# Layer-1 pairs of GpSimd, the order of TensorE's pairs and the spread of the gathers in a recommender tower

## The reference, cut to what matters

```python
e = stack([tbl_f[ids[:, f]] for f in range(32)], axis=1)        # 1024 x 32 x 16
xk = e
for W in (W0, W1, W2):                                           # K = 64 outputs each
    xk = relu(einsum('bmd,bhd,mhk->bkd', e, xk, W)); outs.append(xk.sum(axis=2))
h = concat([*outs, dense_ctx], axis=1)
h = relu(h @ W_top1 + b_top1); h = relu(h @ W_top2 + b_top2); y = h @ W_top3
```

## Time and profile before

| | |
|---|---|
| time, median of 3 runs | 665.63 us (664.72 to 666.06) |
| the profiled execution | 662.89 us, its span 661.1 us, so 1.8 us lie around the span |
| TensorE (PE) busy | 605.5 us (92%) |
| VectorE (DVE) busy | 569.6 us (86%) |
| GpSimd (POOL) busy | 453.1 us (69%) |
| ScalarE (ACT) busy | 358.0 us (54%) |
| mean granted TensorE clock | 0.974 |
| DMA, mean over the span | 181 GB/s |

### The profile page before, as it was taken

The page is one execution under the profiler, slowest core; times in us unless marked ns, Lnnn a source line. Parts: engine busy times, 40 slices in busy tenths (PEclk is TensorE's granted clock), DMA queues, the critical chain, the costliest instruction groups (busy, mean ns, idle before and its releaser), DMA issues. The chain is left out here.

```text
span 661.1 us, 9151 instructions
## 1 busy us (share of the span) xinstructions
PE 605.5 (92%) x3172; PEld 247.5 (37%) x3172; DVE 569.6 (86%) x336; ACT 358.0 (54%) x669; POOL 453.1 (69%) x307
## 2 busy tenths in 40 slices
PE   4499849979999999989999999999999999999988
PEld 3352313224343344424343344434443443434434
DVE  5759975986989899897989899898989898999863
ACT  0184922817647392927647392928556482829251
POOL 6786887888869694888869697787877070716220
PEclk9689969989999999999999999999999999999989
DMA  6899679797695969698694969688795869492000
GB/s 186 190 240 278 150 213 214 217 216 193 146 248 142 208 199 214 193 200 237 141 255 137 213 193 211 193 198 225 180 258 131 186 217 217 155 214 41 1 0 1
DMA packets 60175, 119.82 MB, mean 181 GB/s; under 512 B 15271, under 2 KB 33734, under 8 KB 60054
## 3 DMA queue, kind: packets, MB, share of 16 engines
q1 hardware_dynamic: 41798, 111.02, 67.1%
q10 hardware_dynamic: 10768, 6.53, 3.7%
q0 software_dynamic: 7584, 1.96, 3.0%
HBM read 115.27 MB, written 5.25 MB: 182 GB/s over the span
## 5 line engine op out<-in xcount | busy, mean ns | idle before, releaser
L483 DVE TENSOR_TENSOR z_dve<-xq,x0b 128x2048 f32<-128x2048 f32 x209 | 464.5, 2283 | 68.4 <-ACT xq L637 39.2
L879 PE MATMUL acc<-z_dve,w_cin 128*64 128x512 f32 x1672 | 379.2, 597 | 11.1 <-DVE z_dve L483 10.8
L439 POOL TENSOR_TENSOR z_pool<-x0b,xs 128x2048 f32<-128x2048 f32 x47 | 213.5, 4558 | 108.2 <-ACT xs L637 107.2
L423 POOL DMA_INDIRECT emb<-in_tbl_dram,ids_all x224 | 220.0, 982 | 72.0 <-issue 70.3
L879 PEld LDWEIGHTS acc<-z_dve,w_cin 128*64 128x64 f32 x1672 | 122.4, 137 | 234.9 <-issue 186.5
L645 ACT ACTIVATE xq<-acc 32x512 f32<-32x512 f32 x256 | 144.6, 565 | 3.4
L637 ACT ACTIVATE xq<-acc 64x512 f32<-64x512 f32 x128 | 73.0, 570 | 119.8 <-DVE z_dve L483 62.8
L879 PE MATMUL acc<-z_pool,w_cin 128*64 128x512 f32 x376 | 90.6, 615 | 16.1 <-POOL z_pool L439 16.1
L637 ACT ACTIVATE xs<-acc 64x512 f32<-64x512 f32 x128 | 75.7, 591 | 1.9
L483 DVE TENSOR_TENSOR z_dve<-xq,x_rot 128x2048 f32<-128x2048 f32 x30 | 67.2, 2281 | 0.0
L879 PE MATMUL acc<-z_dve,w_sym 128*64 128x512 f32 x256 | 58.0, 593 | 0.2 <-DVE z_dve L483 0.2
(11 more groups left out here) (97 smaller groups left out, 229.2 us busy)
## 6 DMA issues: line engine op xcount, KB each, us to landing
x0b<-x0t SPq DMA_DIRECT2D x120, 512.0 KB, 14.5
x_rot<-x0t SPq DMA_DIRECT2D x60, 512.0 KB, 6.2
x_rep<-x0t SPq DMA_DIRECT2D x15, 512.0 KB
x0b<-x0t SPq DMA_DIRECT2D x16, 256.0 KB, 7.2
emb<-in_tbl_dram,ids_all POOLq DMA_INDIRECT x224
x0t<-emb_t ACTq DMA_DIRECT2D x28, 128.0 KB
w_cin<-in_L_rec_W_dram SPq DMA_DIRECT2D x16, 64.0 KB
x_lo<-x0t SPq DMA_DIRECT2D x15, 64.0 KB
```

The lines of the kernel that those rows point to most:

```text
L423: nc.gpsimd.indirect_dma_start(out=rows[:, D * f:D * f + D], out_offset=None, in_=tables[f], in_offset=bass.IndirectOffsetOnAxis(ap=ids_al ...
L439: nc.gpsimd.tensor_tensor(z_pool[:, n % ZP_SLOTS, :, :], x0b[b % 2][:, 2 * j:2 * j + 2, :], xs[l - 1][:, :].unsqueeze(1).broadcast_to([P, ...
L483: nc.vector.tensor_tensor(z_dve[:, base % Z_SLOTS, :, :], in0.unsqueeze(1).broadcast_to([P, 2, N]), in1, ALU.mult).then_inc(z_made, 1)
L879: ins = nc.tensor.matmul(acc[l][K * side:K * side + K, :], weights[c], z[:, c, NH * side:NH * side + NH], start=start and c == 0, stop=sto ...
```

## The change

GpSimd has no pair of layer 1 in block 0 and only (NAT, 0) in block 1. Its gathers are spread anew. TensorE takes the SWP pairs of layer 1 first. The waits that count `xs_x1_ready` follow from there being no such write for block 0. Two pieces of tile 1's transposing move in block 0: the second half's transposes to the third pair of layer 2, and ScalarE's `move_half(1, 1)` ahead of `set_relu(1, 0, 0)`.

```diff
     def pool_l1(b):
-        return (3,) if b == 0 else (0, 1)
+        return () if b == 0 else (0,) if b == 1 else (0, 1)
     def gathers(b):
-        return (9, 1, 12) if b == 0 else (0, 14, 8) if b == 1 else (0, 14, 2)
+        return (14, 2, 8) if b == 0 else (3, 9, 6) if b == 1 else (0, 10, 6)
     def l1_order(b):
         if b == 0:
-            return [(NAT, 0), (NAT, 1), (NAT, 2), (SWP, 0), (SWP, 1), (SWP, 2), (NAT, 3), (SWP, 3)]
-        return [(NAT, 0), (NAT, 1), (SWP, 0), (SWP, 1), (SWP, 2), (SWP, 3), (NAT, 2), (NAT, 3)]
+            return [(NAT, 0), (NAT, 1), (NAT, 2), (NAT, 3), (SWP, 0), (SWP, 1), (SWP, 2), (SWP, 3)]
+        if b == 1:
+            return [(SWP, 0), (SWP, 1), (NAT, 0), (SWP, 2), (SWP, 3), (NAT, 1), (NAT, 2), (NAT, 3)]
+        return [(SWP, 0), (SWP, 1), (NAT, 0), (SWP, 2), (NAT, 1), (SWP, 3), (NAT, 2), (NAT, 3)]
...
                 n1, n2, n3 = gathers(b)
-                pool.wait_ge(xs_x1_ready, b + 1)
+                if b > 0:
+                    pool.wait_ge(xs_x1_ready, b)
...
                     if not last:
                         x1_pool(t, k + 1)
+                    if k == 0 and first_tile:
+                        move_half(1, 1)
...
                         x1_swp(t, k + 1)
                         if k == 1:
                             set_relu(0, t, 2)
-                    if k == 0 and first_tile:
-                        move_half(1, 1)
...
             x1_nat(0, 0)
             x1_swp(0, 0)
-            x1_pool(0, 0)
             set_relu(0, 0, 0)
...
                         cin_pair(2, t, k, v, j, i)
-                        if i == 6 and k == 0 and first_tile:
+                        if i == 2 and k == 0 and first_tile:
                             pe.wait_ge(emb_copied, 1)
                             transpose_half(1, 1)
```

More of the change, by code:

```diff
@@ L500, in add_relu @@
                 if l == 0:
-                    dve.wait_ge(xs_x1_ready, 2 * t + 2)
+                    dve.wait_ge(xs_x1_ready, 2 * t + 1)
                     dve.wait_ge(x1_ready[NAT], 2 * t + 2)
@@ L663, in x1_pool @@
                 act.wait_ge(*acc_done(0, t, k))
-                if blk(t, k) > 0:
+                if blk(t, k) > 1:
                     act.wait_ge(*pool_made(1, t, k - 1))
@@ L863, in claim @@
                 if l == 0:
-                    pe.wait_ge(xs_x1_ready, 2 * t + k)
+                    if blk(t, k) > 1:
+                        pe.wait_ge(xs_x1_ready, 2 * t + k - 1)
                     pe.wait_ge(x1_ready[NAT], 2 * t + k)
```

## The result

| | before | after |
|---|---|---|
| time, median | 665.85 us (664.72 to 667.13, 4 runs) | 690.39 us (688.87 to 690.57, 4 runs) |
| span of the profiled execution | 661.1 us | 688.8 us |
| mean granted TensorE clock | 0.974 | 0.960 |

The change makes the kernel slower: the ratio is 1.0373, with a 95% interval of 1.0349 to 1.0396. That is +24.5 us in the medians and +27.7 us between the two profiled executions; the forecast was +19.4. Runs that add a line above these have them one higher.

What follows compares the result with a forecast made beforehand. TensorE, 92% busy and nearly gapless from block 3, was taken as the bound. Opening -8.8, blocks 4, 8, 10, 12 +21.6, block 6 +6.2 and block 14 +0.4 sum to +19.4 on 665.6: 685.0 us, range 671 to 691.

Steps and rivals of the forecast that it cites:

- The opening: Blocks 0 to 2: TensorE's 1.23 and 8.74 us holes go, and -8.8 us remains of all the opening.
- Rival 3: The opening gives nothing because VectorE or a late x0b holds block 1, and the waits stay: 694 us; chance 0.06.
- Place, cause and number of the waits: Even blocks, second half's transposes: the last gather starts 7.5 us later and lands late during the x0b load; 4.3 us wait.
- the sign: In the profile after: waits of 3.5 to 5 us on gathers' DMA, tiles of 77.5 to 79.5 us, half-clock stretches behind each.
- The landing: Time from a gather's start until it lands during the x0b load: 7.8 to 8.7 us, taken as 8.4.
- Rival 1: The gathers land in time, under 4.1 us, so the kernel is faster: 652 us; chance 0.12.
- The slow clock behind each wait: After each wait at the transposes TensorE's clock is lowered: 1.1 us a time, bounded by 0 and 1.7.
- Block 6: GpSimd's 8.04 us stall in block 5 recurs: two late layer-1 pairs, a 4.4 us gather wait and the clock, +6.2 us.
- What was costed at nothing: The pairs' order in layer 1 costs nothing; `move_half(1, 1)` fits in ScalarE's queue, and nothing waits for the SyncE loads it advances.

Runs made afterwards that it cites:

- the filled wait: The changed kernel with ten matmuls of 256 columns on constants ahead of each of the six waits: 678.38 us, against 689.10 for the changed kernel on that chip.
- the last spread of the gathers: The changed kernel with gathers spread (14, 3, 8), (5, 9, 7), (0, 10, 6), 64 ahead of block 2: 718.18 us on the second chip, 647.53 on the third.

## Why the prediction was right, and which term was too small

The forecast was 685.0 us, with 671 to 691 around it; 690.39 is inside, near its upper end. That it is inside is in part luck: the sum itself missed 8.3 us of the 27.7 between the profiled executions, and the forecast's base of 665.6 plus 27.7 would be 693.3, outside. The mechanism is the one that was forecast. The steps in turn:

- **The opening**: the hole of 8.74 us and the one of 1.23 go, as said. Layer 1 of block 1 ends on TensorE at 103.5 us, where 102.7 was forecast, and block 2's at 146.29, where it was 144.8. So -7.3 us remains instead of -8.8. Of the 1.5 us missing, 0.8 is block 1's later end, 0.1 the path from there to the transposes (39.0 us, forecast 38.9), and 0.6 the clock (142.50 to 146.29 is 3.79, forecast 2.14 + 1.1). Rival 3, an opening that gives nothing, is out. (Two of the forecast's sums here are 0.1 us too high: 84.75 + 15.4 + 0.6 is 100.75 and not 100.85, and 66.1 + 2.32 + 2.40 + 4.60 is 75.4. It changes nothing.)
- **Place, cause and number of the waits**: six, in blocks 2, 4, 6, 8, 10 and 12, at the second half's transposes, released by the gathers' DMA. In blocks 4, 8, 10 and 12 they are 4.44, 4.53, 4.58 and 4.43 us, against 4.3 forecast; in block 2 it is 5.06. The tiles of 79.5 to 80.0 us lie above the 77.5 to 79.5 that were named as the sign. The path from the odd block's layer 1 to these transposes was forecast as 38.9 us and took 39.2 (426.56 to 465.79). The landing was taken as 8.4 us, and is 8.8. Rival 1, gathers that land in time, falls in that row.
- **The slow clock behind each wait**: this is the term that was mis-sized. It stood with 1.1 us a time. Each of the four tiles is 6.44, 6.58, 6.70 and 6.15 us longer than before; less its wait that leaves 2.00, 2.05, 2.12 and 1.72, mean 2.0, and the filled wait gives 1.6 to 1.8 in a measurement of its own. I had allowed for a part of the low stretch to fall into the wait and taken the upper bound from a single pair (1.7). In fact next to nothing of it did: from the start of the transposes to that of the pair it is 0.62 us (before: 0.37), and the whole pair behind them ran slowly, 3.5 us to the next start in blocks 4, 8 and 10 and 3.1 in block 12 (before: 1.8). The low clock took in the start of layer 0 too, 4.64 us in block 4 and 3.92 in block 10 for 3.60, but that cost the tile almost nothing: from this row to the next layer 0 it is 36.7 us, against 36.6 before, since TensorE has a wait of 0.7 us for VectorE to give up in layer 2. The clock makes 3.5 of the 4.3 us by which these four tiles exceed the forecast's +21.6; the longer waits make the rest.
- **Block 6**: +8.5 us against the forecast's +6.2. GpSimd's 8 us stall recurred (8.25 us), at the gather that was named. GpSimd was 5.1 us late behind it, as forecast (its two layer-1 pairs start 22.1 us after the start of layer 0 in block 5, at 262.76; those of block 10 start 17.0 us after that of block 9, at 426.56). The late pairs cost less than said, 0.67 and 0.86 us and not 2.8 in all: the slack of each was larger than I took it to be. The wait for the gather is 6.46 us and not 4.4: I had taken its landing to end with the `x0b` load, but it starts at 298.31 and TensorE is released at 305.83, 7.5 us later and some 3 us after that load thins out (DMA share 0.67 in 302 to 304 and 0.18 in 304 to 306, windows of PE). The run with two gathers later supports this: there the load is issued at 285.86 instead of 282.03 and the gather starts 5.5 us later (303.83), and the release comes at 309.49, 23.6 us after the load's issue where it was 23.8. So in this block the landing went by the load and not by its own start. What takes the last 3 us isn't known.

```profile
302.00:304.00 2.00, 0.00 (x0) 0.81 0.67 126
304.00:306.00 2.00, 0.17 (x1) 0.50 0.18 34
```

- **What was costed at nothing**: TensorE's order did cost nothing (0.999 alone). `move_half(1, 1)` moved forward has no run of its own; the only loss seen there is the 0.8 us by which block 1 ends late.

Together: 1.5 us for the opening, 4.3 for the four tiles and 2.3 for block 6 are missing in the forecast. They account for 8.1 us of the 8.3 between +19.4 and the +27.7 of the profiled executions; the medians lie 3.2 us closer together than these two. The term that was too small is thus the clock behind each wait, 2.0 us and not 1.1, with block 6 and the opening behind it.

## What to carry to other kernels

When work that issues DMAs is spread anew, count for each buffer which issue completes it, and put beside that count the landing time as the trace shows it at that place and not the one of an idle moment: here 8.8 us, where packets moved within 2 us with the load cut, turned a spread that looked balanced into six waits, and four gathers more ahead of block 2 turned +24 us into -16. A wait in the middle of dense matmuls costs its own length and the slow clock behind it (some 2 us each here), so a wait of 4.5 us is to be counted as 6.5. An engine that only issues may still be the bound of the stage in which it also computes: the order of TensorE's pairs alone was worth nothing, because GpSimd's own work still held the opening.

## What the runs showed of the hardware

- An indirect gather of 8 KB landed in 8.8 us while one queue kept the 16 DMA engines full, and with that load cut to 16 columns its packets moved within 2 us. In block 6 it still took 7.5 us although the load had thinned out some 3 us before it landed.
- In a wait of 4.58 us the granted clock fell to 0.50 and stayed there until after the next pair; with 4.58 us of matmuls in the same place it stayed at 1.00 and the pair ran at full speed.
- The kernel before took 751.9 us on one chip and 665.9 and 664.9 us on two others, in runs of the same program. In the last spread of the gathers, profiled on two of them, the first layer 0 starts at 65.2 us instead of 39.7, and a tile takes 81.3 us instead of 73.3; cutting the `x0b` load left tiles of 77.3 to 81.8. What differs isn't known.
